# Two low state parts moved to GpSimd and three engine queues reordered in the second half of an attention and recurrence kernel

## The reference

```python
Q = elu(x @ Wq.T + bq) + 1; K = elu(x @ Wk.T + bk) + 1; V = x @ Wv.T + bv
KV = einsum('bnd,bne->bde', K, V)
Z = einsum('bnd,bd->bn', Q, K.sum(axis=1) + 1e-06)
x = layernorm(x + (einsum('bnd,bde->bne', Q, KV) / Z[..., None]) @ Wo.T + bo)
# second block: a recurrence over the 8 sequences, c is (512, 128)
for xt in x:
    f = sigmoid(xt @ wf.T + c @ uf.T + bf); i = sigmoid(xt @ wi.T + c @ ui.T + bi)
    g = tanh(xt @ wc.T + c @ uc.T + bc);    c = f * c + i * g
h = tanh(einsum('tbi,oi->tbo', x, wo) + c @ uo.T + bo)    # every t uses the last c
out = layernorm(x + h)
```

## Time and profile before

| | |
|---|---|
| median of 3 runs | 101.9 us (101.89 to 102.13) |
| profiled execution, its own time | 101.17 us |
| its span, first to last instruction | 99.1 us |
| mean granted TensorE clock | 0.987 of full speed |
| busy: TensorE, VectorE, ScalarE, GpSimd | 89.7, 80.6, 67.1, 38.8 us |
| instructions: TensorE matmul, VectorE, ScalarE, GpSimd | 607, 236, 139, 55 |

### The profile page before, as it was taken

How to read it: one execution, slowest core, us unless ns; L and a number is a source line. 1 busy time by engine, 2 the same in 40 slices (tenths; PEclk the granted TensorE clock), 3 DMA queues, 4 the chain that set the end, 5 groups by cost and what they waited for, 6 DMA issues and landing times.

```text
span 99.1 us, 1905 instructions
## 1 busy us (share of the span) xinstructions
PE 89.7 (91%) x607; PEld 78.1 (79%) x607; DVE 80.6 (81%) x236; ACT 67.1 (68%) x139; POOL 38.8 (39%) x55
## 2 busy tenths in 40 slices
PE   5998999999999999999999999999999999998000
PEld 4768879688588968878898889999999999896000
DVE  3154499979999996899589989999856897999970
ACT  1445779479697694876769445759496678999460
POOL 3006398317258048109505802440200324445750
PEclk9999999999999999999999999999999999999995
DMA  0958999200000000000000000000000003032636
GB/s 24 312 190 310 394 400 374 81 0 3 0 0 0 0 0 0 10 0 0 0 0 0 0 0 7 0 7 0 7 0 0 0 0 106 9 103 100 218 106 212
DMA packets 5413, 7.36 MB, mean 74 GB/s; under 512 B 507, under 2 KB 3228, under 8 KB 5404
## 3 DMA queue, kind: packets, MB, share of 16 engines
q1 hardware_dynamic: 4972, 6.92, 19.3%
q10 hardware_dynamic: 432, 0.33, 1.1%
HBM read 5.15 MB, written 2.10 MB: 73 GB/s over the span
## 4 chain that ended last, share of the span: by engine, by line
PE 75%; DVE 14%; ACT 3%; issue 2%; POOL 1%; DVEq 0%; ACTq 0%
PE ps_k L423 7%; PE ps_ctx L446 7%; PE ps_ctx L466 6%; PE ps_q L437 6%; DVE stats L1177 4%; PE ps_x L480 4%; DVE x L1196 4%; PE ps_f L410 4%; DVE x L1166 2%; PE ps_f L500 2%; PE ps_ctx L456 2%; PE ps_ctx L457 2%; PE ps_f L509 2%; PE ps_c L502 1%; PE ps_c L500 1%
## 5 line engine op out<-in xcount | busy, mean ns | idle before, releaser
L364 POOL TENSOR_TENSOR s_lo<-s,s_hi 128x512 fp32r<-128x512 f32 (+1 forms) x6 | 6.6, 1103 | 24.4 <-ACT s_hi L784 24.4
L332 POOL TENSOR_TENSOR rstd<-var_eps,minus_half 128x4 f32<-128x4 f32 x8 | 8.7, 1090 | 7.8 <-DVE var_eps L983 7.7
L357 POOL TENSOR_TENSOR rstd<-var_eps,minus_half 128x4 f32<-128x4 f32 (+1 forms) x9 | 8.8, 984 | 3.5 <-DVE var_eps L1184 3.3
L992 DVE TENSOR_SCALAR x<-x,stats,rstd 128x128 f32<-128x128 f32 x28 | 9.8, 410 | 0.0
L323 POOL TENSOR_TENSOR k_pair<-k_rows 128x256 f32<-128x256 f32 x8 | 6.3, 784 | 8.9 <-DVE k_rows L1019 8.9
L833 ACT ACTIVATE x_hi<-ps_x 128x512 fp32r<-128x512 f32 x8 | 4.8, 603 | 6.4 <-PE ps_x L480 6.4
L754 ACT ACTIVATE k_exp<-ps_k,minus_one 128x512 f32<-128x512 f32 x8 | 5.5, 686 | 4.6 <-PE ps_k L431 3.8
L423 PE MATMUL ps_k<-wkq,x_cols 128*128 128x128 f32 x64 | 8.6, 278 | 0.0
L437 PE MATMUL ps_q<-x_cols,wkq 128*128 128x512 f32 x16 | 8.2, 593 | 0.0
L423 PEld LDWEIGHTS ps_k<-wkq,x_cols 128*128 128x128 f32 x64 | 7.8, 192 | 0.5 <-DMA wkq<-w_kq 0.4
L1007 DVE SCALAR_TENSOR_TENSOR x<-ps_ctx,z_inv,x_rows 128x128 f32<-128x128 f32 x28 | 8.0, 344 | 0.1
(11 more groups left out here) (209 smaller groups left out, 280.9 us busy)
## 6 DMA issues: line engine op xcount, KB each, us to landing
x_cols<-xt SPq DMA_DIRECT2D x8, 256.0 KB, 7.2
x_rows<-x SPq DMA_DIRECT2D x8, 256.0 KB, 7.2
out<-x SPq DMA_DIRECT2D x7, 256.0 KB, 2.2
wgate<-w_gate SPq DMA_DIRECT2D x1, 384.0 KB, 6.9
out<-x SPq DMA_DIRECT2D x2, 128.0 KB, 2.0
wkq<-w_kq ACTq DMA_DIRECT2D x1, 131.0 KB, 3.7
wvo_in<-w_vo_in ACTq DMA_DIRECT2D x1, 128.0 KB, 3.5
wout<-w_out SPq DMA_DIRECT2D x1, 128.0 KB, 7.0
```

Source lines behind the costliest of these rows:

```text
L332: nc.gpsimd.tensor_tensor(rstd[:, b], var_eps[:, b], minus_half[:], ALU.pow).then_inc(rstd_ok, 1)
L357: nc.gpsimd.tensor_tensor(part_of(rstd, u, T), part_of(var_eps, u, T), minus_half[:, 0:nt * H].rearrange("p (t c) -> p t c", c=H), ALU.pow ...
L364: nc.gpsimd.tensor_tensor(s_lo[:, t % 2, part], state(t)[:, part], s_hi[:, t % 2, part].bitcast(F32), ALU.subtract).then_inc(slo_ok[k], 1)
L992: nc.vector.tensor_scalar(x1[:, b, c], x1[:, b, c], mean_of(b, c), rstd[:, b, c:c + 1], ALU.subtract, ALU.mult).then_inc(x1_ok, 1)
```

## The change

GpSimd makes the low parts of states 9 and 10, which VectorE made. On TensorE `add_g(1)` moves ahead of `gates_s(10)`, `gates_x(11)` ahead of `add_g(2)`, and `out_s(4)` ahead of `out_g(1)`. On VectorE `second_statistics(1)` moves ahead of `second_shift(0)` and `second_statistics(2)` ahead of `step(11)`; from unit 5 on the loop is written out, with the statistics and the variance of unit 7 ahead of unit 5's blocks. VectorE normalises two blocks of unit 5 in place of three, ScalarE two in place of one. The queues of ScalarE and SyncE keep their order.

```diff
-DVE_NORM = [1, 1, 2, 2, 2, 3, 0, 2, 2]
+DVE_NORM = [1, 1, 2, 2, 2, 2, 0, 2, 2]
...
             first_shift(6)
             reciprocal_root(7)
             state_low(6)
+            state_low(9)
             for u in range(len(UNITS)):
                 if u in VAR_BY_POOL:
                     second_variance(u)
                 second_root(u)
+                if u == 0:
+                    state_low(10)
...
             out_s(0)
             out_g(0)
             gates_x(10)
+            add_g(1)
             gates_s(10)
-            add_g(1)
             out_x(2)
+            gates_x(11)
             add_g(2)
-            gates_x(11)
             gates_s(11)
             out_x(3)
             add_g(3)
             out_x(4)
+            out_s(4)
             out_g(1)
-            out_s(4)
             out_x(5)
...
             step(8)
             step(9)
             second_residual(0)
-            state_low(9)
             g_low()
             second_statistics(0)
             step(10)
             second_residual(1)
-            state_low(10)
+            second_statistics(1)
             second_shift(0)
-            second_statistics(1)
             second_residual(2)
             second_normalise(0)
+            second_statistics(2)
             step(11)
             second_shift(1)
-            second_statistics(2)
             second_normalise(1)
             second_residual(3)
             second_statistics(3)
...
             second_shift(3)
             second_normalise(3)
-            for u in range(5, len(UNITS)):
-                if u not in IN_PSUM:
-                    second_residual(u)
-                second_statistics(u)
-                second_variance(u)
-                if DVE_NORM[u - 1] < len(blocks(u - 1)):
-                    second_shift(u - 1)
-                second_normalise(u - 1)
-            second_normalise(len(UNITS) - 1)
+            second_residual(5)
+            second_statistics(5)
+            second_variance(5)
+            second_shift(4)
+            second_normalise(4)
+            second_statistics(6)
+            second_variance(6)
+            second_shift(5)
+            second_statistics(7)
+            second_variance(7)
+            second_normalise(5)
+            second_shift(6)
+            second_statistics(8)
+            second_variance(8)
+            second_normalise(7)
+            second_normalise(8)
```

## The result

The changed kernel takes 102.13 us (median of 22 runs, 101.56 to 102.56), the kernel before 101.85 us beside it (22 runs, 101.03 to 102.28): ratio 1.0042 with a 95% interval of 1.0022 to 1.0062 (the ratio is not the quotient of the two medians, which is 1.0027). In a second series, with twelve runs of the changed kernel beside 35 of the kernel before, the ratio was 1.0067 (1.0036 to 1.0098). It is slower, by 0.2 to 0.6 us in the first series and 0.4 to 1.0 in the second; the forecast was 0.6 (a ratio of 1.0059), and both intervals hold it. The times of the first series alone would not tell these two apart; the profiles do.

What follows compares the result with a forecast made beforehand. VectorE, busy 4.86 of 5 us from 85 to 90 us, was taken to bound the kernel. Residual 4 0.62 late less 0.05 in the tail gave 0.57, about 0.6: 101.9 + 0.6 = 102.5 us, range 102.05 to 102.9.

Steps and rivals of the forecast that it cites:

- Step 10: TensorE's `add_g(1)` ahead of `gates_s(10)`: its 0.48 of matmuls makes the tanh start at 77.95 against 77.59, 0.36 late.
- The tanh of unit 2: ScalarE's `out_tanh(2)`, waiting for `add_g(2)` behind `gates_x(11)`: starts at about 81.07 against 80.21, 0.86 late.
- Step 11: ScalarE's unit 0 blocks come late, so this step's tanh starts at 82.9 against 82.06, 0.84 late.
- TensorE's wait for GpSimd's second low part: Before `gates_s(11)` ends: some 0.4 of waiting, covered by 0.3 to 0.5 because ScalarE arrives only at 82.9.
- Residual 3: On VectorE, 0.84 late less 0.69 for unit 2's statistics moved earlier: starts at 85.36, only 0.15 late.
- The late out_g(1): Behind `out_s(4)` on TensorE, it delays ScalarE's `preload(5)` and `out_tanh(4)`, then VectorE's unit 4 residual: 0.45 more.
- The tail: After unit 6's statistics: ScalarE's blocks follow the end of unit 6's root by 0.24 instead of 0.29, giving 0.05.
- The sum: Whole kernel: 0.62 late at unit 4's residual less 0.05 at the end, 0.57 slower, about 0.6.
- A slow low part: Rival, 6%: GpSimd's 128x256 low part takes 1.3 instead of 0.73, losing 0.3 more: 102.8.
- Root 6 holding VectorE's blocks: Rival, 4%: GpSimd's unit 6 root and VectorE's unit 5 blocks exclude each other; end 0.5 later, 103.0.
- VectorE's saved work coming through: Rival, 5%, faster: `out_tanh(2)` starts by 80.3, the residuals of units 3 and 4 come 0.69 earlier: 101.2.
- The absorbed `out_g(1)`: Rival, 12%: ScalarE reaches `out_tanh(4)` by 86.9 or state 11 comes 0.5 earlier; no measurable change, 102.0.

## Why the prediction was right

The direction, the chain and the size held. By its steps, on the clock of before:

- *Step 10, forecast 0.36 late.* It came 0.47 late (78.06). This is the term that was mis-sized. The two matmuls of `add_g(1)` were priced at 0.48 as they stood back to back in the earlier trace rows. In the new place the second waits for `g_low`, and behind a wait it holds TensorE from 78.01 to 78.35, 0.34 and not 0.24. In the kernel with the low parts back the same pair is again 0.34 apart. The row of a matmul that had waited was in the earlier trace rows (0.39 in place of 0.28) and was used for the latency alone.
- *The tanh of unit 2, forecast 81.07:* 81.19, this 0.1 carried on. That it and shift 0 meet at the blocks of unit 0 was right (81.82 against 81.73 forecast), and the run with `add_g(2)` back shows that the second way alone suffices.
- *Step 11, forecast 0.84 late:* 0.93. TensorE's wait for GpSimd's second low part was forecast as some 0.4: the matmul started 0.40 later than 0.12 behind the one ahead of it (the row counts 0.24 of it as idle time), and this was hidden as forecast.
- *Residual 3, forecast 0.15 late:* 0.26, the 0.1 again.
- *The late out_g(1), forecast 0.45 of idle time of VectorE:* 0.41 by the row and 0.41 by the run with the order undone. Residual 4 came 0.75 late against 0.62: state 11 brings 0.09 of this, and `out_s(4)` 0.12, since it held TensorE 87.11 - 86.12 = 0.99 and not the 0.87 of eight such matmuls that hadn't waited; the rows behind it gave some 0.08 back. This is the same mis-sizing as in step 10, a group of matmuls that starts behind a wait.
- *The tail, forecast to give 0.05:* from the statistics of unit 6 to ScalarE's blocks 94.18 - 91.74 = 2.44 before and 95.68 - 93.34 = 2.34 after, so 0.10. The gap behind the root's end is 0.23 in place of 0.29, as forecast (0.24). The other 0.04 is the root itself, 1.07 long (1071 ns by the group of 94.3 to 95 us) and not 1.11, which the forecast had left as it was. Undoing the order costs at most 0.04.
- *The sum, forecast 0.57:* 0.75 - 0.10 = 0.65, by the stretches 0.66. What it lacks is 0.13 at the residual of unit 4, the two matmul groups behind a wait above all, less the 0.05 more that the tail gave.
- *The rivals.* A slow low part: both took 0.73. Root 6 holding VectorE's blocks: GpSimd's roots ran from 94.38 to 96.05 and VectorE's two blocks of unit 5 began inside, at 94.81, and took 0.59, as two such blocks do elsewhere. What the Trainium skill says of the shared port (SBUF — State Buffer, Who interferes with whom) does not show here either, for a root that reads four values per partition; whether these blocks ran in a two-port mode no row says. VectorE's saved work coming through: the statistics moved ahead of step 11 were worth what was said (step 11 is 0.93 late and residual 3 only 0.26), but step 11 was too late for it. The absorbed `out_g(1)`: VectorE's 0.41 of idle time refutes it.

The median of the changed kernel came out at 102.13 and not at 102.5, though the path was right. The first series gives 0.28 between the medians and 0.42% (0.43 us) by the ratio, and not 0.66; the upper end of its interval, 0.63 us, stays just below the stretch's 0.66, while the second series (0.67%) agrees with it. Why the first is lower is not shown. The start of the kernel varies by up to 1 us from execution to execution, as follows, and that 102.13 lies within the range owes something to the range's width.

## What to carry to other kernels

Work put ahead of a pass to fill a short wait can cost far more than the wait: TensorE waited some 0.1 us, `add_g(1)` held it for 78.35 - 77.75 = 0.60 us in that place, and step 10 came 0.39 us later than in the same kernel with the `add_g` orders of before. Price such a filling by rows of instructions that had waited, not by rows that stood back to back. In queues that are strictly in order, look at what stands behind a wait without needing it: the tanh of unit 4 behind `preload(5)`, and step 11 behind the blocks of unit 0, were worth 0.4 and 0.5 us. Where the runs of a kernel spread more than the effect, compare profiles from the last common point ahead of the change; that distance repeated within 0.02 us in the two kernels that were profiled twice.

## What the runs showed of the hardware

**The start is what varies.** The eight first matmuls of the first keys, which begin at 4.5 to 4.6 us, took 1.05 to 1.91 us in the thirteen profiles that can be used, and the first tanh of unit 0 followed: 75.33 where they took 1.05, 75.58 at 1.38, 75.76 at 1.53, 76.02 at 1.79, 76.31, 76.35 and 76.36 at 1.91; one profile departs from this by 0.15 (76.16 at 1.90), and there the 512-column matmul that follows took 0.58 where it took 0.77 in the three with 1.91. The groups by shape, window 5.1 to 5.4 us, of the kernel before and the changed one:

```profile
L423 PE MATMUL ps_k<-wkq,x_cols 128*128 128x128 f32 x5 | 0.7, 275 | 0.0
```

```profile
L426 PE MATMUL ps_k<-wkq,x_cols 128*128 128x128 f32 x3 | 0.8, 418 | 0.0
```

The mean of one matmul is 418 ns in place of 275. The granted clock reads 1.00 in both windows, so the record doesn't name the cause; it was not tested. So the mean of the profile's clock, 0.987 and 0.992, says nothing of this.

**One execution with TensorE at about a fifth of its speed.** In the profiled execution of the kernel with the tanh of unit 4 first, TensorE was busy for 494.4 us against 89.7 in the kernel before, slow from its first matmul to its last, with a granted clock of 1.00. The groups by shape of that execution and of the kernel before:

```profile
L426 PE MATMUL ps_k<-wkq,x_cols 128*128 128x128 f32 x64 | 45.1, 1047 | 0.0
```

```profile
L423 PE MATMUL ps_k<-wkq,x_cols 128*128 128x128 f32 x64 | 8.6, 278 | 0.0
```

The other engines kept their durations (a tanh of 128x256 took 0.47). It happened once in all runs of this study, and its cause is open.
